# Causal masks on VectorE and the q/k projections inside the layernorm loop, in a two-layer kernel on 8 cores

## The reference

```python
def _L0_attn_ref(x, Wq, bq, Wk, bk, Wv, bv):      # x is the layernormed input
    q = jnp.einsum('bse,hde->bshd', x, Wq) + bq
    k = jnp.einsum('bse,hde->bshd', x, Wk) + bk
    v = jnp.einsum('bse,hde->bshd', x, Wv) + bv
    mask = jnp.triu(jnp.full((s, s), -jnp.inf, dtype=x.dtype), k=1)
    scores = (jnp.einsum('bqhd,bkhd->bhqk', q, k) + mask) * inv_scale
    attn = jax.nn.softmax(scores, axis=-1)
    out = jnp.einsum('bhqk,bkhd->bqhd', attn, v)
    return out.reshape(b, s, h * hd)
```

## Time and profile before

| | us |
|---|---|
| median of 2 runs | 6356.32 |
| the two runs | 6339.90 and 6372.73 |
| profiled execution, its own time | 6332.55 |
| its span on the slowest core (core 1) | 6331.0 |
| spans of the 8 cores | 6316.8 to 6331.0 |
| granted TensorE clock, mean of each core | 0.749 to 0.752 |
| attention stage: layernorm to about | 148 |
| q and k projections to about | 262 |
| v projection to about | 318 |
| first load of the next stage | 2030 |
| TensorE busy, of the span | 3493.8 (55%) |
| VectorE busy | 1954.4 (31%) |
| ScalarE busy | 1251.5 (20%) |
| GpSimd busy | 967.3 (15%) |

### The profile page before, as it was taken

The page is one execution under the profiler, slowest core; times in us unless marked ns, Lnnn a source line. Parts: engine busy times, 40 slices in busy tenths (PEclk is TensorE's granted clock), DMA queues, the critical chain, the costliest instruction groups (busy, mean ns, idle before and its releaser), DMA issues.

```text
span 6331.0 us, 45811 instructions; the slowest of 8 cores (6316.8 to 6331.0 us)
## 1 busy us (share of the span) xinstructions
PE 3493.8 (55%) x15560; PEld 1483.8 (23%) x15560; DVE 1954.4 (31%) x3013; ACT 1251.5 (20%) x2020; POOL 967.3 (15%) x731
## 2 busy tenths in 40 slices
PE   1912222333443026664028156633999999999993
PEld 1400000000001013333013022211444444444441
DVE  2122223223101547677542311223221122212223
ACT  1211111221332112221000321103112211121111
POOL 0033333332221222232220000000000000000000
PEclk9955555555555558887559588875999999999997
DMA  4000000000000010000115412163033113113214
GB/s 97 1 20 33 28 30 35 28 30 35 15 5 24 30 34 14 27 14 10 37 44 161 105 27 20 20 174 83 7 47 54 23 31 54 27 27 54 34 20 153
DMA packets 139218, 271.18 MB, mean 43 GB/s; under 512 B 41424, under 2 KB 74704, under 8 KB 137968
## 3 DMA queue, kind: packets, MB, share of 16 engines
q0 software_dynamic: 99840, 127.73, 11.1%
q1 hardware_dynamic: 36848, 132.13, 6.1%
q10 hardware_dynamic: 2304, 8.39, 0.4%
HBM read 299.33 MB, written 53.48 MB: 56 GB/s over the span
## 4 chain that ended last, share of the span: by engine, by line
PE 47%; DVE 17%; POOL 11%; ACT 9%; DMA 8%; issue 6%; DVEq 3%; ACTq 0%; POOLq 0%; SPq 0%
PE pq L1590 14%; PE pq L1562 14%; PE pq L1217 4%; DMA a_wrowA<-wgu 2%; POOL a_expB L412 2%; PE pq L427 2%; ACT a_expA L400 2%; POOL a_expA L409 2%; PE pq L279 2%; PE pq L385 2%; POOL b_q L553 2%; ACT a_expB L401 2%; PE pq L429 1%; PE pq L874 1%; POOL b_hb L556 1%
## 5 line engine op out<-in xcount | busy, mean ns | idle before, releaser
L1562 PE MATMUL pq<-d_tT,d_w1e 128*128 128x512 bf16 x4096 | 898.5, 382 | 34.5 <-ACT d_hTh L1572 34.5
L1590 PE MATMUL pq<-d_w2e,d_hTh 128*128 128x512 bf16 x4096 | 889.2, 379 | 33.7 <-ACT d_hTh L1572 33.7
L427 PE MATMUL pq<-a_expA,a_vsb 128*65 128x512 bf16 x320 | 194.4, 608 | 1087.3 <-POOL a_expB L412 806.9
L1606 DVE SCALAR_TENSOR_TENSOR d_acc<-pq,d_comb,d_acc 128x512 f32<-128x512 f32 x256 | 192.2, 751 | 1423.8 <-PE pq L1590 1423.8
L1572 ACT ACTIVATE d_hTh<-pq,d_b1s 128x512 bf16<-128x512 f32 x512 | 351.6, 687 | 1225.0 <-PE pq L1562 1225.0
L1562 PEld LDWEIGHTS pq<-d_tT,d_w1e 128*128 128x128 bf16 x4096 | 402.1, 98 | 527.0 <-issue 50.9
L1590 PEld LDWEIGHTS pq<-d_w2e,d_hTh 128*128 128x128 bf16 x4096 | 398.5, 98 | 524.3 <-issue 48.5
L400 ACT ACTIVATE a_expA<-pq 128x512 bf16<-128x512 f32 x320 | 190.9, 596 | 1193.9 <-PE pq L389 1193.9
L526 DVE TENSOR_REDUCE a_blkA<-a_wrowA 128x64 f32<-128x1024 f32 x44 | 53.7, 1220 | 1058.9 <-DMA a_wrowA<-wgu 1058.9
L1217 PE MATMUL pq<-c_xn2T,c_wsl 128*128 128x512 bf16 x1024 | 263.3, 403 | 162.3 <-ACT c_ga L1227 81.6
L427 PEld LDWEIGHTS pq<-a_expA,a_vsb 128*65 128x65 bf16 x320 | 41.8, 131 | 1239.6 <-issue 1239.6
(11 more groups left out here) (218 smaller groups left out, 4116.5 us busy)
## 6 DMA issues: line engine op xcount, KB each, us to landing
d_w1e<-w1T POOLq DMA_DIRECT2D x32, 1024.0 KB, 9.3
d_w2e<-w2T POOLq DMA_DIRECT2D x8, 4096.0 KB, 27.3
a_wrowA<-wgu POOLq DMA_DIRECT2D x44, 512.0 KB, 3.8
b_xt<-x SPq DMA_DIRECT2D x32, 512.0 KB, 4.7
wq_pre<-a_qbfA POOLq DMA_DIRECT2D x44, 256.0 KB, 2.4
b_wdr<-wd SPq DMA_DIRECT2D x8, 1408.0 KB, 6.0
a_xt<-x SPq DMA_DIRECT2D x16, 512.0 KB, 3.6
s<-a_s0c SPq DMA_DIRECT2D x16, 512.0 KB, 2.6
```

Source lines behind the costliest of these rows:

```text
L427: p.te.matmul(pq[4][0:65, :], vA, expA[:, esl * 512:(esl + 1) * 512], start=(kc == 0), stop=(kc == nkc - 1))
L1562: inst = p.te.matmul(bank[:], w1e[:, j * MOE_H + hc * 128: j * MOE_H + (hc + 1) * 128], tT[:, j * S + hf * 512: j * S + (hf + 1) * 512], s ...
L1590: inst = p.te.matmul(bank[:], hTh[:, j * 512 + tr * 128: j * 512 + (tr + 1) * 128], w2e[:, j * D + dh * 512: j * D + (dh + 1) * 512], star ...
```

## The change

Two edits, both in the attention stage.

The q and k projections leave their place behind the layernorm loop and go into it, as `emit_qkv(qt)`, issued after every fourth token tile for the query tile just finished. The order of the groups is now query tile, then q or k, then head pair. They use banks 6 and 7 in turn instead of 0 and 1, and TensorE waits for the copy of the block's last token tile instead of the loop's last.

The masks of the last four key chunks of a pass go from GpSimd to VectorE, and TensorE waits for VectorE's semaphore in place of GpSimd's. Nothing else in the loop is changed, `emit_wq_unit` and its place included.

```diff
+        def emit_qkv(qt):
+            p.te.wait_ge(p.ved.h, ve_evac[qt * 4 + 3])
+            for which, dst, bias, scl in (("q", qT, bqs, 0.125),
+                                          ("k", kT, bks, 1.0)):
+                base = 0 if which == "q" else D
+                for hp in range(NP):
+                    bank = pq[6 + len(se_qkv) % 2]
+                    if len(se_qkv) >= 2:
+                        p.te.wait_ge(p.sed.h, se_qkv[-2])
+                    for j in range(ND):
+                        inst = p.te.matmul(
+                            bank[:],
+                            wT_c(j, base + hp * 128, base + hp * 128 + 128),
+                            xnT_c(j)[:, qt * 512:(qt + 1) * 512],
+                            start=(j == 0), stop=(j == ND - 1))
+                    inst.then_inc(p.ted.h, 1)
+                    te_mm = p.ted.bump()
+                    p.se.wait_ge(p.ted.h, te_mm)
+                    if not se_qkv:
+                        p.se.wait_ge(p.ved.h, ve_init)
+                    p.se.activation(dst[:, hp * S + qt * 512: hp * S + (qt + 1) * 512],
+                                    bank[:], AF.Identity, bias=bias[:, hp:hp + 1],
+                                    scale=scl).then_inc(p.sed.h, 1)
+                    se_qkv.append(p.sed.bump())
+
         for i in range(NT):
...
             ve_evac.append(p.ved.bump())
+            if i % 4 == 3:
+                emit_qkv(i // 4)
         ve_xnT = ve_evac[-1]
-        p.te.wait_ge(p.ved.h, ve_xnT)
-        se_qkv = []
-        for which, dst, bias, scl in (("q", qT, bqs, 0.125), ("k", kT, bks, 1.0)):
-            base = 0 if which == "q" else D
-            for hp in range(NP):
-                for qt in range(4):
-                    bank = pq[len(se_qkv) % 2]
...
                     if masked:
                         mi = kc - (nkc - 4)
-                        p.gp.wait_ge(p.sed.h, se_exp[kc])
-                        p.gp.tensor_tensor(expA[:, esl * 512:(esl + 1) * 512],
+                        p.ve.wait_ge(p.sed.h, se_exp[kc])
+                        p.ve.tensor_tensor(expA[:, esl * 512:(esl + 1) * 512],
                                            expA[:, esl * 512:(esl + 1) * 512],
                                            masks[:, mi * 512:(mi + 1) * 512], ALU.mult)
-                        p.gp.tensor_tensor(expB[:, esl * 512:(esl + 1) * 512],
+                        p.ve.tensor_tensor(expB[:, esl * 512:(esl + 1) * 512],
                                            expB[:, esl * 512:(esl + 1) * 512],
                                            masks[:, mi * 512:(mi + 1) * 512], ALU.mult) \
-                            .then_inc(p.pod.h, 1)
-                        pod_mask = p.pod.bump()
-                        p.te.wait_ge(p.pod.h, pod_mask)
+                            .then_inc(p.ved.h, 1)
+                        ve_mask = p.ved.bump()
+                        p.te.wait_ge(p.ved.h, ve_mask)
```

More of the change, by code:

```diff
@@ L204, in narrative, with xnT_c, wT_c @@
         ve_evac = []
+        se_qkv = []
+        def xnT_c(j):
+            return xnT[:, j * S:(j + 1) * S]
+        def wT_c(j, c0, c1):
+            return wT[:, j * 3 * D + c0: j * 3 * D + c1]
+        def emit_qkv(qt):
[22 more added lines that the diff above has]
+                    se_qkv.append(p.sed.bump())
         for i in range(NT):
```

## The result

The changed kernel takes 5986.1 us (median of 11 runs), the kernel before 6342.63 us (median of 10 runs). The ratio is 0.9416, with a 95% interval of 0.9381 to 0.9451. In a part of the executions some cores run at a lower granted clock, in the dense later stages and on some cores in the projections too; the ratios leave these out, and where a few microseconds decide, the attention stage is read in the trace, on a core that starts its value projection within 2 us of the changed kernel's. The profiled execution took 5976.28 us, 356 us less than the 6332.55 us of the one before. The forecast of 5950 us was 36 us too quick, inside its range of 5905 to 6038. The sum had given 5946 us for a profiled execution, 30 us too quick.

What follows compares the result with a forecast made beforehand. Attention was taken as a chain of waits, chiefly for GpSimd's masks. Gains of 192 (masks) and 208 (queue) less 8 (contention) and 6 (projections) made 386 us: 5946 from 6332.55 profiled, forecast 5950, range 5905 to 6038.

Steps and rivals of the forecast that it cites:

- The sum: Whole kernel: 192 + 208 - 8 - 6 = 386 us off the profiled 6332.55 us, giving 5946 us.
- What bounds the kernel: Attention: a chain of waits, with TensorE idle 1087 us before the value product, 806.9 us of it ended by GpSimd's mask.
- The pair of masks: Masked chunks in attention: a pair takes 0.76 us on VectorE instead of 2.26 on GpSimd, 128 times, 192 us gained.
- the quick bound: Masks on VectorE: two elements in a cycle, 425 ns for 512 columns; the slow bound was 692 ns.
- The queue: Between attention passes: next masks wait behind VectorE's heads only, not GpSimd's load, head, tail and store; 208 us gained.
- heads at T+0: T ends a pass's last mask pair; VectorE's weight-quantizing head starts there, not at T+3.8 (tile 0) or T+3.72 (tile 1).
- second heads of a pair: Tile 1, two weight units behind each pass: the second head starts at T+18.43 instead of T+22.15.
- the loads ahead: Weight loads in attention: GpSimd, without masks, issues them early; in tile 0 landed 2.7 us before the pass ends.
- Contention: GpSimd's tail beside the first masks after a head: 0.4 us lost in each of 21 passes, 8 us.
- mask B: The second mask of a pair, which under a whole hold would wait for GpSimd's L553, 1.9 us long.
- Rival 2: Masks behind a head: VectorE shut out by GpSimd's tail, 2 us x 21 = 42 us, 5980 us; 8 in 100.
- The projections: q and k blocks in the layernorm loop: TensorE and layernorm still alternate, three times 2.0 us, 6 us lost.

Runs made afterwards that it cites:

- `b1_load_behind`: The changed kernel, with GpSimd waiting for the pass's last mask before it issues a weight unit's load: 6214.7 us in one run.
- `a3b_small_tail`: The changed kernel, with GpSimd's tail of a weight unit in attention replaced by one 16-column operation and a memset: 5905.78 us in one run.
- `a4_one_mask`: The changed kernel, with one VectorE operation of 2 x 512 columns in place of the two masks: 5964.13 us in its quickest run.

## Why the prediction was right, and where it was off

**What bounds the kernel.** Right. TensorE waited for masks; its busy time and clock in the last query tile did not change, and 355 us of its wait for masks went.

**The pair of masks** (192 us). Right: 0.42 us an operation, 0.76 a pair, at the quick bound; tile 3 shows the 1.5 us a pair by itself. The choice by the bf16 copy in the earlier trace rows held, and so did the Trainium skill's double rate for bf16 `tensor_tensor` (VectorE: DVE Perf Modes, The perf-mode tier table), which the trace of before could not show.

**The queue** (208 us). Right in its parts: heads at T+0, second heads of a pair at T+18 to 19, the loads ahead in all tiles. `b1_load_behind` gives the price of the early load alone, 86/21 = 4.1 us a pass where 3.7 were reckoned.

**Contention** (8 us taken, 42.4 measured). This is the term that was mis-sized, and it is nearly the whole of what the sum missed. The step that failed is "VectorE loses 0.2 us" from L491 in the earlier trace rows. The overlap in that row was 0.32 us long (610.04 to L553's end at 610.36), so 0.2 us was no sign of sharing. Read against the overlap it is a full hold: in the changed kernel L417 was held from 344.14 to L558's end at 346.01, 1.87 us, and lost 2.15 - 0.42 = 1.73: 0.14 us of the hold do not show in its length, and no run here tells why. The same 0.14 off the overlap of L491, 0.32 - 0.14 = 0.18 us, is what L491 lost. L556 in the same rows was held from 610.50 to L491's end at 611.44, 0.94 us, and lost 0.82. Both rows already said that each excludes the other whole. So does the next L491 in the timeline of before, which the prediction does not use:

```profile
613.21 1.53 DVE L491 TENSOR_TENSOR a_s0c<-a_s0c,a_rsum 128x1024 f32<-128x1024 f32 x1
616.50 1.23 DVE L491 TENSOR_TENSOR a_s0c<-a_s0c,a_rsum 128x1024 f32<-128x1024 f32 x1
```

It stood against L556 for 0.45 us (to 613.66) and lost 0.30, and the one behind it met nothing and took 1.23. Between the two overlaps, 0.13 us more of overlap cost 0.13 us more: no share of it came free. I had written "at worst its whole overlap" and then priced the overlap of the earlier trace rows, when what mattered was the length of the overlap in the changed kernel: mask B would stand against 1.9 us of L553.

**Rival 2** had this mechanism right, with its place, 2 us a pass and 5980 us, and was given 8 in 100 for the same misreading. The measured time is nearer to it than to the forecast; that it lies inside the range is owed to the range having been drawn around the rivals, not to the contention term. The Trainium skill (SBUF — State Buffer, SBUF: two separate sides) states the rule that the runs bear out: whichever of the two starts first keeps the pair of ports for the whole operation. `a3b_small_tail` (reading operation of 16 columns, 0.02 us lost) and `a4_one_mask` (order turned round, GpSimd held instead) show it here.

**The projections** (6 us lost). Right in sign and mechanism, too large: 2 to 3 us. From block to block it takes 52.3, 52.2 and 51.9 us instead of 53.5. Blocks take 28.8 to 30.2 us instead of 30.7, since TensorE came to the quick pace sooner than in the earlier trace rows (the third eviction starts 6.5 to 7.8 us behind the start of its block, there 8.28), and a tile in between takes 5.5 to 5.9 us, where the 5.96 of my mean held one slow tile.

**The sum.** Forecast 5946, measured 5976. The hold adds 34 us and the projections take 3 to 4 off. About 5 us more come from the ends of tiles: an output copy L478 stands 2.1 to 2.4 us for the store two back, at most 0.4 before. It goes with GpSimd's load of 512 KB issued between those stores, which before was not issued there. `b1_load_behind` bears this out, though it was made for something else: with the load issued later, the same wait is 0.39, 0.99 and 0.93 us at the three tile ends.

```profile
502.67 1.40 DVE L496 TENSOR_TENSOR a_s0c<-a_s0c,a_rsum 128x1024 f32<-128x1024 f32 x1
...
507.45 0.54 POOL L348 DMA_DIRECT2D a_wrowA<-wgu  x1
...
512.61 0.43 DVE L478 COPY a_s0c<-pq 128x260 f32<-128x260 f32 x1 [2.25 <-DMA s<-a_s0c]
```

These terms make 35 us where 30 were missed; I have no cause for the 5 us between them. The two profiled executions of the changed kernel, 5976.28 and 5983.12 us, differ by 7.

## What to carry to other kernels

When work moves to another engine, list what it no longer stands behind and what it now stands behind; here the engine that was relieved issued its loads early, 95 us of the 356, and nothing in the diff said so. A loss read from an overlap means nothing until it is set against the length of that overlap: divide before you call it small. And work that is moved into a loop to overlap does so only if it stands in the in-order queues in pieces short enough for the loop's own chain to go on between them; four groups a tile gained 65 us where sixteen groups a block lost 2 to 3.

## What the runs showed of the hardware

VectorE operations with two inputs in SBUF and GpSimd operations that read SBUF exclude each other whole, in either order: 2.15 us instead of 0.42 for a mask behind L558, 2.24 instead of 1.92 for GpSimd's operation behind a mask. A VectorE copy out of PSUM is not held: L476 in the earlier trace rows starts while L553 runs and takes the 0.42 us of the copy ahead of it. A single VectorE operation of 2 x 512 bf16 columns whose second input is the same 512 columns read twice keeps the double rate (0.68 us, where 1024 f32 columns take 1.225).
